# A selective-scan and expert kernel: the prologue reordered, one expert's weight pieces split there, and a projection moved two places back in the loop

## What is computed

```python
xp, res = split(x @ W_in.T, 2)                 # 512 channels each
xc  = silu(conv4(xp) + conv_b)                 # four taps along the sequence
B, C, dt = split(xc @ W_x.T)                   # 16, 16 and 1 numbers a token
dt  = softplus(dt @ W_dt.T + b_dt)
h_t = exp(A * dt_t) * h_(t-1) + dt_t * B_t * xc_t     # 16 states for each channel
y_t = sum over states of h_t * C_t  + D * xc_t
x   = layernorm(x + silu(y + res) @ W_out.T)
# then: router, top 2 of 8 experts (256 -> 1024 -> 256, exact gelu), weighed sum, layernorm
```

## Time and profile before

| | us |
|---|---|
| median of 3 runs | 1629.46 (1626.07 to 1636.35) |
| the profiled execution, its own time | 1632.02 |
| its span in the trace | 1630.4 |
| PE, DVE, ACT, POOL busy | 1337.3, 1188.2, 1041.5, 957.0 |
| first scan to last scan | 61.0 to 990 |
| granted TensorE clock, mean | 0.908 |

### The profile page before, as it was taken

How to read it: one execution, slowest core, us unless ns; L and a number is a source line. 1 busy time by engine, 2 the same in 40 slices (tenths; PEclk the granted TensorE clock), 3 DMA queues, 4 the chain that set the end, 5 groups by cost and what they waited for, 6 DMA issues and landing times. The chain is left out here.

```text
span 1630.4 us, 29176 instructions
## 1 busy us (share of the span) xinstructions
PE 1337.3 (82%) x8770; PEld 1113.3 (68%) x8771; DVE 1188.2 (73%) x2115; ACT 1041.5 (64%) x1438; POOL 957.0 (59%) x847
## 2 busy tenths in 40 slices
PE   4598898888888988988987895459999999999940
PEld 1367577676577677667676784349889899889840
DVE  2679888888798788788886895536666666666648
ACT  3798996997986987987987873123333333333324
POOL 0288877778877888877889885512222222222227
PEclk7699899999999899999999897579999999999975
DMA  2032222222322323322323226242443612311135
GB/s 97 13 99 82 78 85 91 91 75 92 103 75 97 96 75 101 98 83 87 99 65 98 97 85 213 82 132 95 155 137 102 209 65 71 125 37 40 41 110 212
DMA packets 91047, 158.44 MB, mean 97 GB/s; under 512 B 11664, under 2 KB 38928, under 8 KB 90960
## 3 DMA queue, kind: packets, MB, share of 16 engines
q1 hardware_dynamic: 75856, 125.30, 23.9%
q0 software_dynamic: 9888, 27.29, 5.0%
q10 hardware_dynamic: 5216, 4.74, 0.8%
HBM read 108.64 MB, written 48.65 MB: 96 GB/s over the span
## 5 line engine op out<-in xcount | busy, mean ns | idle before, releaser
L1027 POOL TENSOR_TENSOR arena<-arena 128x1024 f32<-128x1024 f32 x256 | 614.2, 2405 | 71.4 <-DVE arena L802 60.4
L403 PE MATMUL d_ps<-ident,arena 128*128 128x128 f32 x2048 | 338.8, 292 | 66.3 <-DVE arena L802 60.2
L403 PEld LDWEIGHTS d_ps<-ident,arena 128*128 128x128 f32 x2048 | 257.4, 150 | 196.6 <-DVE arena L802 96.6
L802 DVE TENSOR_TENSOR_SCAN arena<-arena,carry,d_ps 128x512 f32<-128x512 f32 x256 | 320.5, 1271 | 72.9 <-PE d_ps L403 69.4
L624 ACT ACTIVATE arena<-u_tok,b_tok 128x512 f32<-128x512 f32 x512 | 327.7, 715 | 65.6 <-PE d_ps L403 61.3
L802 DVE TENSOR_TENSOR_SCAN arena<-arena,d_ps 128x512 f32<-128x512 f32 x256 | 305.1, 1211 | 79.9 <-PE d_ps L403 67.5
L416 PE MATMUL y_ps<-ident,arena 128*128 128x128 f32 x2048 | 310.6, 282 | 41.2 <-POOL arena L1027 41.2
L1255 POOL DMA_INDIRECT expert_out<-y,dest x71 | 71.1, 1001 | 371.0 <-PE xt_ps L1309 322.7
L416 PEld LDWEIGHTS y_ps<-ident,arena 128*128 128x128 f32 x2048 | 249.3, 147 | 47.2 <-POOL arena L1027 47.2
L1285 ACT ACTIVATE h_t<-ht_ps 128x512 f32<-128x512 f32 x142 | 84.5, 595 | 296.6 <-PE ht_ps L1340 296.6
L635 ACT ACTIVATE arena<-dt,neg_a 128x2048 f32<-128x2048 f32 x128 | 255.8, 1999 | 1.3 <-DVE arena L802 0.7
(11 more groups left out here) (168 smaller groups left out, 1605.0 us busy)
## 6 DMA issues: line engine op xcount, KB each, us to landing
arena<-c_rows SPq DMA_DIRECT2D x128, 256.0 KB
weight_parts<-arena SPq DMA_DIRECT2D x80, 256.0 KB
arena<-weight_parts SPq DMA_DIRECT2D x20, 1024.0 KB
arena<-in_pieces SPq DMA_DIRECT2D x80, 128.0 KB
xg<-expert_rows POOLq DMA_DIRECT2D x71, 130.0 KB, 2.4
c_y<-expert_out SPq DMA_DIRECT2D x16, 512.0 KB, 7.8
arena<-in_pieces SPq DMA_DIRECT2D x12, 512.0 KB, 7.1
x_t<-in_x_t SPq DMA_DIRECT2D x8, 512.0 KB, 4.9
```

Source lines behind the costliest of these rows:

```text
L403: last = nc.tensor.matmul(d_ps[:, c % 2, j * P:(j + 1) * P], ub[:, g % U_RING, j, c * P:(c + 1) * P], t.ident[:], start=True, stop=True, i ...
L802: nc.vector.tensor_tensor_scan(h[:, g % H_RING, c, :], decay[:, g % D_RING, c, :], d_ps[:, c % 2, :], 0.0 if i % 2 == 0 else carry[:, n, c ...
L1027: nc.gpsimd.tensor_tensor(h[:, g % H_RING, lo:hi, :], h[:, g % H_RING, lo:hi, :], c_row[:, g % C_RING:g % C_RING + 1, :].broadcast_to([P, ...
```

## The change

1. `setup`: the load of W_in is cut into its two halves; only the first, with the input's block 0, is waited for by the first product. That input is issued by ScalarE's queue, the second half comes later in SyncE's. TensorE runs 24 products of 128x128 into a tensor that nobody reads, once GpSimd's masks are made.
2. Expert 7's 16 pieces are split in the prologue, as four parts of 128x1024: load, cast on ScalarE (`first_part`), subtraction on GpSimd (`first_rest`), store. They lie in the buffers of `h`; the first scan waits for the four stores. `PIECE_STEPS` loses steps 9 and 11, so the loop splits 64 pieces, eight in a block.
3. ScalarE's programs of iterations -2 and -1 are written out anew: `first_part(0)` stands ahead of the first reading of the in-projection; the second reading of z (the Relu of the step sizes) is replaced by VectorE's work on a second copy of z (`spread_z2`, `first_sizes`), and so is the copy of B; the exponential of A and the decay of step 0 come ahead of u; the input of step 0 is made from PSUM (`first_scale`) ahead of the copies of u.
4. TensorE runs unread products in iteration -1: 14 at (2, 0) and 20 at (12, 2) (`keep_running`).
5. In every iteration the two products of `in1` move from (11, 1) and (11, 2) to (11, 3) and (12, 0).

```diff
@@ setup
+        first = [(t.w_in[:, :, 0:INNER], w_in[:, :, 0:INNER])]
+        early = [(t.x_t[:, 0], d.x_t[0])]
...
+        @block.tensor
+        def _(pe):
+            pe.wait_ge(pool_done, 8)
+            for _ in range(24):
+                nc.tensor.matmul(idle_ps[:], t.ident[:], t.before[:], start=True, stop=True)
@@ pieces
-        PIECE_STEPS = (0, 1, 3, 4, 6, 8, 9, 10, 11, 12)
-        PARTED = (EXPERTS - W_RING) * PIECES
+        PIECE_STEPS = (0, 1, 3, 4, 6, 8, 10, 12)
+        PARTED = (EXPERTS - W_RING - 1) * PIECES
@@ SyncE, before its iterations
+            for m in range(FIRST_PARTS):
+                sp.dma_start(first_parts[:, m, :, 1], d.pieces[last, m * FIRST_PIECES:(m + 1) * FIRST_PIECES]
+                             .rearrange("q p n -> p q n")).then_inc(first_raw[m], 16)
             for k in range(PARTS_RING):
                 sp.dma_start(parts[:, k, 1], raw_piece(k)).then_inc(raw_loaded[k], 16)
+            for m in range(FIRST_PARTS):
+                sp.wait_ge(first_low, m + 1)
+                hold(sp, held_sp)
+                sp.dma_start(d.parts[last, m * FIRST_PIECES:(m + 1) * FIRST_PIECES]
+                             .rearrange("q p h n -> p q h n"), first_parts[:, m]).then_inc(first_stored, 16)
@@ TensorE
+                def keep_running(count):
+                    for _ in range(count):
+                        nc.tensor.matmul(d_ps[:, 0, :], t.w_in[:, 0, 0:P], x_t[:, 0, 0, :], start=True, stop=True)
...
+                    if i == -1 and at == (2, 0):
+                        keep_running(14)
+                    if i == -1 and at == (12, 2):
+                        keep_running(20)
...
-                        if at in ((11, 1), (11, 2)):
-                            in_projection(1, q - 1)
+                        if at in ((11, 3), (12, 0)):
+                            in_projection(1, 0 if n == 11 else 1)
@@ ScalarE
+            def first_scale(j):
+                wait_filled(act, f"ut{j}", 0)
+                nc.scalar.activation(ub[:, 0, j, :], bank(f"ut{j}", 0), ACT.Identity,
+                                     scale=b_tok[:, 0, j, 0:1]).then_inc(scaled, 1)
...
+                if i == -2:
+                    first_part(0)
+                    for c in range(EC):
+                        xp_out(c)
+                    first_part(1)
+                    first_part(2)
+                    return
+                if i == -1:
+                    silu()
+                    act.wait_ge(t.rest_loaded, 16 * REST_LOADS)
+                    first_part(3)
+                    ssm_out()
+                    for c in range(EC):
+                        z_parts(c)
+                    soft_tail()
+                    nc.scalar.activation(t.neg_a[:], t.neg_a[:], ACT.Exp).then_inc(exp_done, 1)
+                    decays(0)
+                    xp_out(0)
+                    xp_out(1)
+                    wait_freed(act, "btok", 0)
+                    for j in range(TT):
+                        first_scale(j)
+                    for j in range(TT):
+                        ut_out(j)
...
+                    scale(1)
+                    decays(1)
+                    xp_out(2)
+                    xp_out(3)
+                    return
@@ VectorE (scan: before step 0; f == 0 alone: the rest)
+                            dve.wait_ge(first_stored, 16 * FIRST_PARTS)
...
+                def first_sizes():
+                    wait_filled(dve, "z2", f)
+                    for c in range(EC):
+                        last = nc.vector.tensor_scalar(dt[:, f % 2, c, :], bank("z2", f), t.w_dt[:, c:c + 1],
+                                                       t.b_dt[:, c:c + 1], ALU.mult, ALU.add)
...
+                        nc.vector.scalar_tensor_tensor(out=dt[:, f % 2, lo:hi], in0=dt[:, f % 2, lo:hi], scalar=0.0,
+                                                       in1=pre[:, lo:hi], op0=ALU.max, op1=ALU.add).then_inc(dt_done, 1)
@@ GpSimd, before its iterations
+            for m in range(FIRST_PARTS):
+                first_rest(m)
```

More of the change, by code:

```diff
@@ L53, in setup @@
                 (t.neg_a, d.a_log.partition_broadcast(P)),
-                (t.d_col, d.d_skip), (t.x_t[:, 1], d.x_t[1]),
+                (t.w_in[:, :, INNER:2 * INNER], w_in[:, :, INNER:2 * INNER]), (t.d_col, d.d_skip), (t.x_t[:, 1], d.x_t[1]),
                 (t.w_out, d.w_out.rearrange("(c p) n -> p c n", p=P)),
                 (t.router, d.router.rearrange("(k p) n -> p k n", p=P))]
-        assert (len(first), len(taps), len(rest)) == (FIRST_LOADS, TAP_LOADS, REST_LOADS)
+        assert (len(first) + len(early), len(taps), len(rest)) == (FIRST_LOADS, TAP_LOADS, REST_LOADS)
         @block.sync
@@ L92 @@
 BANK_OF = {"turn0": 0, "turn1": 1, "logits": 0, "ssm": 1, "yt0": 0, "yt1": 0, "z": 1, "yt2": 0, "yt3": 0,
-           "out0": 0, "ranks": 1, "out1": 1, "btok": 0, "in0": 0, "in1": 1, "ut0": 0, "ut1": 1, "ut2": 0, "ut3": 1,
+           "out0": 0, "ranks": 1, "out1": 1, "z2": 2, "btok": 0, "in0": 0, "in1": 1, "ut0": 0, "ut1": 1, "ut2": 0, "ut3": 1,
            "in2": 0, "in3": 1}
@@ L114, in bank_counts @@
             b = i + BLOCK_OF[u]
-            if 0 <= b < BLOCKS:
+            if 0 <= b < BLOCKS and (u != "z2" or b == 0):
                 fills[bank_of(u, b)] += 1
@@ L152, in mamba @@
         h = view(H_RING, EC, T)
+        assert EC * T == PIECES // 4 * 2 * PW and H_RING >= 4
         assert U_RING * TT * INNER + EC * T == PIECES * 2 * PW
@@ L256, in mamba @@
         w_low = sem("w_low")
+        first_raw = [sem(f"first_raw{m}") for m in range(4)]
+        first_high = sem("first_high")
+        first_low = sem("first_low")
+        first_stored = sem("first_stored")
         high_done = sem("high_done")
@@ L471, in spread_z, with spread_z2 @@
                         .then_inc(m_filled[bank_of("z", f)], 1)
+                def spread_z2():
+                    wait_bank(pe, "z2", f)
+                    nc.tensor.matmul(bank("z2", f), t.ones[2 * STATE:2 * STATE + 1, :],
+                                     ssm[2 * STATE:2 * STATE + 1, :], start=True, stop=True)\
+                        .then_inc(m_filled[bank_of("z2", f)], 1)
                 def turn_u(j):
@@ L563, in between @@
                         spread_z()
+                        if f == 0:
+                            spread_z2()
                     if scans:
@@ L641, in high_part, with first_part @@
                     .then_inc(high_done, 1)
+            def first_part(m):
+                act.wait_ge(first_raw[m], 16)
+                nc.scalar.copy(first_parts[:, m, :, 0].bitcast(F32R), first_parts[:, m, :, 1]).then_inc(first_high, 1)
             def own_high(m):
```

49 lines of the change are left out of this document (40 added, 9 removed).

## The result

| | us |
|---|---|
| before, median of 20 runs of this comparison | 1635.11 (1626.07 to 1642.07) |
| after, median of 20 runs | 1626.87 (1615.27 to 1632.89) |
| ratio after / before, 95% interval | 0.9946 [0.9926, 0.9965] |
| the profiled execution of after, its own time | 1619.12 |
| its span; granted TensorE clock | 1617.5; 0.927 |

By the ratio the change gains 8.8 us, 0.54%; the medians differ by 8.2. The forecast was a gain of 20.6, to 1609, in a range of 1598 to 1622: the measured median, 1626.9, lies above the range, though single runs come down to 1615. The two profiled executions differ by 12.9 us (1632.02 and 1619.12). I cut both traces at the first scan of each step, as for the earlier trace rows, and went through the differences in order.

The account below looks back on a forecast made before the run. No engine is full in the loop, so only what ends last in a step pays; the prologue is one chain. -14.0 - 3.5 - 3.1 = -20.6 us, from a median of 1629.5 to 1609, range 1598 to 1622.

Parts of the forecast that it names:

- the prologue: Up to VectorE's tap behind in2's reading: +4.0 - 2.7 + 0.2 - 4.6 = -3.1 us, between -8 and +4.
- The projection moved back: Step 11 of blocks 1 to 5 gains 16.5 us, step 12 loses 2.5: net -14, bounds -5 to -17.
- VectorE would be late next: Step 11 then lasts as long as VectorE: 8.0 us in blocks 2 to 5, 6.9 in block 1.
- (a): Another engine takes most of step 11's gain, leaving about -6 of the -14: 1617 us; chance 0.18.
- (d): The wait for the residual moves with in1's product, some 3 us more per block: 1649 us; chance 0.04.
- Two pieces fewer: In step 10, GpSimd's multiplication by C starts sooner: 0.5 us in each of seven blocks, -3.5, between +4 and -8.
- the 14 products (28 records, 3 us) at 21: In the prologue, the first unread set ends at 21 us, before silu at 29.9; small projection stays slow, 5.87 us.
- the 20 products, which end some 3 us before u: In the prologue, the second unread set ends before u, leaving the clock up for its turnings; -4.6 us rests on this.
- From u's end to the tap: ScalarE's work from u's end to in2's reading and the tap takes 11.0 us in place of 15.6: -4.6.
- (b): The prologue loses: part's load late behind the constants, low clock for u's turnings, +4 in place of -3: 1616; chance 0.12.
- (e): Unread products don't keep the clock up: already forecast for the first set, 2 us for the second; no chance given.
- (c): A larger gain than forecast, taking -8 for step 10; chance 0.08.

Follow-up runs that it names:

- e4: The kernel before with only in1's two products moved to (11, 3) and (12, 0): median 1620.08 us, ratio to before 0.9900.
- e3: The changed kernel with in1's two products put back to (11, 1) and (11, 2): median 1637.88 us, ratio to before 1.0014.
- e7: The changed kernel with expert 7's pieces split in the loop again, no prologue parts, no second unread set, first set 9: 1615.25 us, ratio to before 0.9890.
- e2: The changed kernel with 4 unread products at (12, 2) in place of 20: median 1613.15 us, ratio to before 0.9871.
- e11: The changed kernel with its 14 and 20 unread products cut to 128 columns each: median 1611.84 us, ratio to before 0.9864.
- e1: The changed kernel without the 20 unread products at (12, 2): median 1613.99 us, ratio to before 0.9866.
- e5: The changed kernel without both sets of unread products in iteration -1, setup's kept: median 1618.49 us, ratio to before 0.9867.
- e10: The kernel before, unaltered, profiled once more: one run, 1636.45 us.
- e6: The changed kernel without setup's 24 unread products and the second set, first set 10 in place of 14: median 1606.16 us, ratio to before 0.9851.
- e8: The changed kernel with unread products cut to 9 in setup, 8, 3 and 7 later, and first_part(0) behind the in-projection's readings: 1604.92 us, ratio to before 0.9824.
- e9: The changed kernel, unaltered, measured and profiled once more: median 1620.36 us, ratio to before 0.9938.

## Why the prediction was wrong, and where it was right

The distance is 1626.9 - 1609 = 17.9 us. It is 10.4 for the prologue, less 2.3 by which the loop did better and 0.5 that the terms leave over, in the traces; 5.6 because the median of three runs from which I started, 1629.46, lay under that of twenty, 1635.11; and 4.7 between the two profiled executions and the medians (12.9 against 8.2). So 10 of it are spread between runs, which no step of the prediction could have named; but with a gain of 20.6 from 1635.1 the forecast would have been 1614.5, still 12 too low.

**The projection moved back: right.** -14 net was forecast; after, e4 and e3 give -15.8 to -16.3. That VectorE would be late next was right; its busy time came down too, and the 6.9 to 8.0 us I took for a step were 6.35 to 7.73. In step 12 I had 0.5 for each of five blocks; it was 0.3 to 0.4 there and 0.9 in block 0. Rivals (a) and (d) fall by e4: neither GpSimd nor the wait of the earlier trace rows took anything back.

**Two pieces fewer: right in the loop, not in the sum.** -3.5 forecast, -4.0 found, +4.0 back in e7. What follows the piece started sooner. GpSimd's timeline of before, step 10 of block 4:

```profile
602.18 2.38 POOL L1027 TENSOR_TENSOR arena<-arena 128x1024 f32<-128x1024 f32 x1
```

The multiplication by C starts 2.50 us behind the start of VectorE's first product there and 1.81 in after (596.88 - 595.07), and VectorE's second product ends 1.08 us behind it in both. I booked the other side, the first reading 4.0 us later through `first_part(0)`, in the prologue's term, but e7 shows that the two belong together and roughly cancel.

**The prologue: the step that failed is "the 14 products (28 records, 3 us) at 21" and "the 20 products, which end some 3 us before u".** I took them as 128 columns wide. Their moving operand is `x_t[:, 0, 0, :]`, 512 tokens: 12.18 us and 17.33 us. The first set therefore overran silu by 1.0 us and yet gave 2.25 back, since it closed the idle gap that I had left open (5.87 became 3.62). The second overran u by 13.4 us. From u's end to the tap I had counted 11.0 us; it was 23.7 in after (73.30 - 49.60), and 10.7 in e2 and e11, whose sets end in time (60.33 - 49.64, 62.31 - 51.62). e11 has the width alone changed and gives the forecast back to 0.5 us. So the cause is shown by a run, and it was no behaviour of the chip: the row that I used, 3.62/8 = 0.45 us for 512 columns, gives 12.6 and 18.1 us for the two sets. The first would have ended 0.5 after silu and saved 2.25; the second, begun 7.4 before u (3 and its own 40 x 0.11), would have ended 10.7 after it: -3.1 + 0.5 - 2.25 + 10.7 = +5.9, near the +7.35 that came.

The other steps of the prologue held. The engines left `setup` at 10.84 (forecast 10 to 11). The part's load landed 4.0 us after its issue and not 4.9, so the first reading was at 15.85 (forecast 16.8, "16 to 17"). u ended at 49.60, 0.8 sooner than in before; the forecast had it 1.5 later (+4.0 - 2.7 + 0.2), and the sooner landing and the gain of the clock make up the difference. No rival had the time: (a), 1617, and (b), 1616, are both some 10 us under the median. Rival (b) named the prologue, with +4, but by a late load and a low clock; the load was early (4.0 us) and the clock high (1.00 in u's turnings). Rival (e), the unread products don't keep the clock up, falls for the sets as they are (1.00 in the small projection and in the turnings), and is right for the first one at 128 columns (e11, 0.56). Of (c), the larger gain, no run shows the -8 that it took for step 10, where 4.0 was found; the small projection at the high clock gave 2.25 (5.87 to 3.62).

Of the range: it had 4 us above for the prologue and no case in which filling TensorE itself comes in the way, though every such product stands ahead of real work in one program. That rival should have stood there, with its price: whatever the set overruns, one for one.

## What to carry to other kernels

Work that only keeps an engine running is priced like any other: take its shape from the operands in the code, its duration from a row of that shape, and compare its end with the moment at which the work behind it could start. Here 40 records cost 13 us, 8 did all that they were for, and the overrun of 13.4 us was far more than the clock could give back there (1.7 us). A product that waits for a bank belongs behind those in the same program that don't need the bank; here that one line gave 16 us and needed nothing of the rest.

## What the runs showed of the chip

**Two lengths of the final sum.** From the last product of the experts to the end, all profiled executions take either about 60.4 us (before, after, e1 to e5, e7, e10, e11) or about 52.5 (e6, e8, e9), the same kernel both: after and e9 are one program. Groups by line in the last 60 us, after and then e9:

```profile
L1624 POOL TENSOR_TENSOR c_rstd<-c_var,minus_half 128x2 f32<-128x2 f32 x16 | 16.9, 1056 | 3.6 <-DVE c_var L1658 3.6
L1657 DVE TENSOR_SCALAR c_var<-c_mv 128x2 f32<-128x2 f32 x16 | 14.3, 895 | 0.5
```

```profile
L1624 POOL TENSOR_TENSOR c_rstd<-c_var,minus_half 128x2 f32<-128x2 f32 x16 | 11.3, 707 | 0.3 <-DVE c_var L1658 0.3
...
L1657 DVE TENSOR_SCALAR c_var<-c_mv 128x2 f32<-128x2 f32 x16 | 5.0, 315 | 0.6
```

Operations on two columns take 895 ns in one and 315 in the other on VectorE, 1056 and 707 on GpSimd. What makes it the one or the other, no run shows. It is worth 8 us of an execution, and may be a good part of what the runs of one kernel differ by.

**Who starts first in step 9.** After and e9 are one program, and block 6 starts at 752.6 in both; it takes 115.6 us in after and 121.1 in e9. 1.9 of the difference lies in step 9 (9.80 and 11.67). Timelines of VectorE and GpSimd there, after and then e9:

```profile
821.79 1.20 DVE L932 TENSOR_TENSOR dt<-dt,pre 128x1024 f32<-128x1024 f32 x1
...
821.93 3.29 POOL L1141 TENSOR_TENSOR arena<-arena 128x1024 f32<-128x1024 f32 x1
```

```profile
823.23 2.79 DVE L932 TENSOR_TENSOR dt<-dt,pre 128x1024 f32<-128x1024 f32 x1
...
822.55 2.38 POOL L1141 TENSOR_TENSOR arena<-arena 128x1024 f32<-128x1024 f32 x1
```

Here whoever starts first takes its usual time, 1.20 or 2.38, and the other 0.91 (3.29) or 1.59 (2.79) more than its own. In blocks 2, 4 and 6 of the 13 profiled executions VectorE was first 29 times, with a step 9 of 9.8 us, and GpSimd ten times, with 11.6 to 12.1; in blocks 1, 3 and 5 GpSimd was always first, with 11.1 to 12.0. So a start that differs by half a microsecond is worth 2 us of a step. What shifts the start, and whether it can be held on the good side, no run here shows.

**VectorE beside GpSimd in e8.** Timelines of VectorE and GpSimd:

```profile
19.15 6.80 DVE L1032 TENSOR_SCALAR diag_d<-ident,d_col 128x128 f32<-128x128 f32 x4
```

```profile
16.38 6.98 POOL L1155 TENSOR_TENSOR arena<-arena 128x1024 fp32r<-128x1024 f32 x3 [13.87 <-ACT arena L701]
23.52 2.35 POOL L1155 TENSOR_TENSOR arena<-arena 128x1024 fp32r<-128x1024 f32 x1 [0.17 <-ACT arena L701]
```

Four operations of 128x128 take 6.80 us while GpSimd subtracts the parts; in after, where no subtraction runs beside them, they take 0.86. The last of them ends at 25.95, 0.08 us after the last subtraction. They stood off the path here, since VectorE waited for silu and z next.
